# One image's turn in another order: new places for each stage on TensorE, VectorE, ScalarE, GpSimd and the DMA queue

## The chip, the core and the metric

The kernel runs on one core of one Trainium2 chip. The metric is device time in microseconds (us) of one execution. The kernel before was run three times: median 4677.69 us, from 4676.67 to 4680.09. The profile is of another execution of the same program.

## What is computed

32 images of 96 channels and 56 x 56 pixels (3136 tokens) go through two layers. Cut to what matters:

```python
# layer 0
h = conv7x7_depthwise(x) + conv_b                    # first phase of the kernel
h = layernorm_over_channels(h)
x = x + layer_scale * (gelu(h @ w1 + b1) @ w2 + b2)  # 96 -> 384 -> 96
# layer 1
t = tokens(x)
h = relu(bn1(layernorm(t) @ aw1))                    # 96 -> 192
X = fft(h, axis=tokens)
xr = relu(X.real * rd - X.imag * idg + rb)
xi = relu(X.imag * rd + X.real * idg + ib)
t = t + bn2(ifft(xr + 1j * xi).real @ aw2)           # 192 -> 96
t = t + quantized_ffn(layernorm(t))                  # 96 -> 384 -> 96, fp8 products
```

The transform over 3136 tokens is done as two small ones (112 x 28), with a store to DRAM and a load back between them in each direction.

## The kernel before

A first phase (the first 640 us) does the convolution for all images and leaves its output in DRAM; the change does not touch it. The second phase, `image_phase`, is a pipeline over images. One pass of its loop is called a **turn**. In turn n, three images are in work at once: part 1 of image n, part 2 of image n-1, part 3 of image n-2, and the start of image n+1. An image is cut into 7 chunks of 448 tokens (8 chunks in part 2). I write M2/0 for stage M2 of chunk 0. The stages, with the lines of TensorE and of the engine that takes the result:

| part | stages in order, with what the other engines do for them |
|---|---|
| next image | L0S statistics (DVE L809), L0N normalize (DVE L831 h_norm), HT transpose (PE L980, ACT L733) |
| 1 | M1 (PE L987, GELU on ACT L748), M2 (PE L993, residual sum with `x_sb` on DVE L853), T transpose and statistics (PE L999, DVE L809), W1 (PE L1007, ReLU on DVE L875), A outer transform (PE L1015, ACT L756, stored by SP L636) |
| 2 | B inner transform (PE L1026, ACT L767, DVE L892, POOL L712), W (PE L1035, ACT L776), IB inner inverse (PE L1042, ACT L741, stored by SP L655) |
| 3 | AP outer inverse (PE L1049, sum on DVE L903), S2 transpose and statistics (PE L1056, ACT L781, DVE L809), N2 normalize (DVE L831 xn), T2 (PE L1062, ACT L789), F1 (PE L1070, ACT L796), G ReLU and cast (DVE L922, L929), F2 (PE L1077, ACT L801, DVE L934 and L939) |

GpSimd (POOL L683) computes the power that ends each statistics step.

Within a turn the program of every engine is a fixed list. Table `STAGES` gives each stage a first place, a distance from chunk to chunk and a count; `LATER` shifts a stage for one engine; `stages` sorts the steps of each engine by these numbers. Nothing else decides the order: semaphores make a step wait for its data and buffers, and everything behind a waiting step on its engine waits too. TensorE's list also decides which of the 8 PSUM banks each result gets (`banks`).

All DMAs of this phase are issued by one queue, SP, whose list is sorted in the same way. Its steps are: M2 (store the chunk to DRAM, L613), A (store the outer transform, L636), IB (store the inner inverse, L655), FETCH and FETCH NEXT (load `t1_old` for AP, L598). Three larger transfers hang on the last chunk of a step. Behind A/6, SP waits for all stores of A and loads `inner`, the input of the next turn's B, 2016 KB and 336 KB and 42 KB (L646, L647). Behind IB/7 it waits for the stores of IB and loads `back` for the next turn's AP (1176 KB, L665). Behind M2/6 it loads the next image into `x_sb` (1176 KB, L594):

```python
if name == "M2":
    sp.wait_ge(t1_done.sem, t1_done.at(n, c))
    sp.dma_start(t1_dram[...], t1[:, c % 4, :])
    if followed and c == NC - 1:
        load_x()
```

`x_sb` is a single buffer, so its load can start only when M2/6 of this turn is done on DVE. Its first reader is M2/0 of the next turn on DVE, which waits for the load:

```python
if name == "M2":
    if c == 0:
        dve.wait_ge(x_loaded.sem, x_loaded.at(n))
```

At the end of a turn SP stores `out` (L670), and at the start of the next it loads `h` (1176 KB, L605). The turns are start, first, second, a loop of 29 equal turns ("steady"), last, after and end.

Of the kernel before, what the change touches and what calls it, by code (L numbers as in the profile page):

```python
# [20 lines left out]
NC = NQ // CH  # L21
# [3 lines left out]
ND = (NS + CH - 1) // CH  # L25
# [50 lines left out]
def before(n, k, per, ring):  # L76

    if k >= ring:
# [3 lines left out]


STAGES = {
    1: {"M1": (-3, 11.8, NC), "M2": (7, 11.8, NC), "T": (13, 11.8, NC), "W1": (22, 11.8, NC), "A": (27, 11.8, NC)},
    2: {"B": (11, 9.3, ND), "W": (24, 9.3, ND), "IB": (28, 8.8, ND)},
    3: {"AP": (3, 11.5, NC), "S2": (8, 11.5, NC), "N2": (14, 11.5, NC), "T2": (18, 11.5, NC), "F1": (20.5, 12, NC),
        "G": (25, 11.5, NC), "F2": (32, 11.5, NC)},
    "next": {"L0S": (34, 3.4, NC), "L0N": (72, 3.3, NC), "HT": (79, 2.8, NC)},
    "fetch": {"FETCH": (9, 11.5, NC - 3)},  # L90
    "fetch next": {"FETCH NEXT": (78, 1, 3)},
}

LATER = {
    "act": {"W": -0.5, "G": -0.5},
    "dve": {"B": 3, "M2": 2, "T": 2, "W1": 1, "F2": 2, "AP": 1, "S2": 1, "L0N": -1, "W": -2},
    "pool": {"B": 4, "T": 3, "S2": 2, "F1": 1},
    "sp": {"M2": 3},
    "pe": {},
}  # L100

# [1233 lines left out]
```

## Time and profile before

| what | us |
|---|---|
| median of three runs | 4677.69 |
| the profiled execution, its own time | 4678.17 |
| its span, first to last instruction | 4676.4 |
| convolution phase, about | 640 |
| 29 turns of the loop, each | 122.85 |
| PE busy, share of the span | 3989.9 (85%) |
| DVE busy, share of the span | 3461.5 (74%) |
| ACT busy, share of the span | 2285.2 (49%) |
| POOL busy, share of the span | 1390.6 (30%) |

The turn's length is the distance from the first to the last pass of the loop at the store of `out`, over 28. Turns of the loop repeat to a few hundredths of a microsecond, so one turn can be read for all; the text reads the one from about 2056 to 2179 us. Matmuls overlap in the pipeline, so PE's busy time is not work at its peak. Lines of the changed kernel are one higher than those given here, because its table has one line more.

### The profile page before, as it was taken

The numbers are of one execution on the slowest core, as the hardware profiler recorded it, in microseconds if no ns is written. First come the engines' busy times: TensorE is split into PE (matmuls) and PEld (weight loads), VectorE is DVE, ScalarE is ACT, GpSimd is POOL, SyncE is SP. The second block draws the span as 40 slices with busy tenths as digits, with TensorE's granted clock in tenths as the row PEclk, the third lists the DMA queues.
The fourth block names the chain that finished last, engine by engine and source line by source line (L and its number), as shares of the span: only waits on it lengthen the run. The fifth ranks groups of instructions, "written<-read, shape, count | busy, mean of one in ns | idle before, by whom it ended". The sixth has DMA issues, their size and how long they took to land.

```text
span 4676.4 us, 88192 instructions
## 1 busy us (share of the span) xinstructions
PE 3989.9 (85%) x22802; PEld 2808.8 (60%) x22802; DVE 3461.5 (74%) x11833; ACT 2285.2 (49%) x4610; POOL 1390.6 (30%) x1572
## 2 busy tenths in 40 slices
PE   5999969888888888888888888888888888888885
PEld 3444436666666666666666666666666666666664
DVE  2333346788888888888888888888888888888876
ACT  2444424455555555555555555555555555555543
POOL 1111233333332333333333333333333232333331
PEclk8999979999999999999999999999999999999986
DMA  6666524344444444444443333343444444444331
GB/s 172 166 169 172 163 71 107 94 111 115 111 113 113 111 112 115 109 113 115 110 114 105 98 102 107 102 108 105 108 113 114 111 113 114 112 112 113 100 91 49
DMA packets 420416, 532.48 MB, mean 114 GB/s; under 512 B 220047, under 2 KB 378493, under 8 KB 404413
## 3 DMA queue, kind: packets, MB, share of 16 engines
q1 hardware_dynamic: 405920, 510.40, 40.6%
q10 hardware_dynamic: 14272, 20.04, 1.7%
q14 instruction: 199, 1.63, 0.1%
q8 instruction: 25, 0.41, 0.0%
HBM read 295.18 MB, written 235.12 MB: 113 GB/s over the span
## 4 chain that ended last, share of the span: by engine, by line
PE 36%; DVE 30%; issue 12%; ACT 2%; POOL 2%; DVEq 1%; DMA 1%; ACTq 0%; POOLq 0%; SPq 0%
PE psum L993 9%; PE psum L987 7%; PE psum L1026 5%; DVE minus L892 5%; DVE xn L831 4%; DVE h_norm L831 4%; DVE plus L892 4%; DVE stats L809 3%; PE psum L1035 2%; PE psum L1007 2%; DVE act L875 2%; PE psum L1015 2%; PE psum L1049 2%; DVE h L922 1%; PE psum L1062 1%
## 5 line engine op out<-in xcount | busy, mean ns | idle before, releaser
L683 POOL TENSOR_TENSOR scales<-sums,minus_half 112x4 f32<-112x4 f32 (+1 forms) x480 | 636.6, 1355 | 2191.8 <-DVE sums L824 2191.8
L712 POOL TENSOR_TENSOR both<-plus,minus 96x224 f32<-96x224 f32 (+1 forms) x1024 | 618.2, 623 | 587.3 <-DVE minus L892 502.9
L993 PE MATMUL psum<-hid,w_sb 128*96 128x448 f32 x1344 | 592.8, 580 | 6.5 <-ACT hid L748 2.0
L987 PE MATMUL psum<-hn,w_sb 96*128 96x448 f32 x1344 | 557.2, 547 | 8.4 <-ACT h L796 6.9
L767 ACT ACTIVATE uw<-psum,spec 96x224 f32<-96x224 f32 (+1 forms) x1024 | 445.6, 511 | 157.5 <-PE psum L1026 154.9
L386 PE MATMUL c_psum<-c_xt,c_toeplitz 128*112 128x448 f32 x1152 | 476.6, 551 | 50.3 <-ACT c_xt L328 26.9
L414 DVE TENSOR_SCALAR c_h<-c_psum,c_bias 112x448 f32<-112x448 f32 x192 | 199.0, 1036 | 413.1 <-PE c_psum L386 413.1
L892 DVE SCALAR_TENSOR_TENSOR plus<-psum,spec,uw 96x224 f32<-96x224 f32 (+1 forms) x1024 | 426.8, 417 | 63.5 <-ACT uw L767 63.0
L748 ACT ACTIVATE hid<-psum,b_sb 128x448 f32<-128x448 f32 x672 | 419.7, 635 | 104.1 <-PE psum L987 61.9
L892 DVE SCALAR_TENSOR_TENSOR minus<-psum,spec,uw 96x224 f32<-96x224 f32 (+1 forms) x1024 | 425.8, 416 | 0.0
L1035 PE MATMUL psum<-aw_sb,both 96*112 96x96 f32 x3712 | 410.3, 263 | 4.7 <-ACT hid L748 4.7
L1026 PE MATMUL psum<-inner_dft,inner 112*96 112x112 f32 x3712 | 404.1, 261 | 4.8 <-DMA inner<-outer_spectrum 4.8
L1035 PEld LDWEIGHTS psum<-aw_sb,both 96*112 96x112 f32 x3712 | 395.3, 179 | 19.6 <-ACT hid L748 17.8
L1026 PEld LDWEIGHTS psum<-inner_dft,inner 112*96 112x96 f32 x3712 | 389.0, 165 | 23.1 <-issue 14.0
L875 DVE SCALAR_TENSOR_TENSOR act<-psum,scales,below 112x192 f32<-112x192 f32 x896 | 309.2, 406 | 96.4 <-PE psum L1007 88.6
L1062 PE MATMUL psum<-ident,xn 112*96 112x112 f32 x896 | 138.4, 282 | 278.8 <-DVE xn L831 278.8
L1007 PE MATMUL psum<-aw_sb,t 96*112 96x192 f32 x1792 | 343.6, 329 | 35.2 <-DVE t L853 35.1
L987 PEld LDWEIGHTS psum<-hn,w_sb 96*128 96x128 f32 x1344 | 246.2, 191 | 211.6 <-issue 154.8
L993 PEld LDWEIGHTS psum<-hid,w_sb 128*96 128x96 f32 x1344 | 218.5, 176 | 245.7 <-issue 220.6
L809 DVE BATCH_NORM_STATS2 stats<-t_rows 112x6 f32<-112x96 f32 x896 | 164.5, 246 | 253.6 <-ACT t_rows L781 253.6
L1007 PEld LDWEIGHTS psum<-aw_sb,t 96*112 96x112 f32 x1792 | 291.8, 177 | 95.4 <-DVE t L853 53.6
L1015 PE MATMUL psum<-act,outer_dft 113*114 113x192 f32 x1792 | 332.3, 328 | 19.1 <-DVE act L875 19.1
(85 smaller groups left out, 6549.5 us busy)
## 6 DMA issues: line engine op xcount, KB each, us to landing
outer_spectrum<-outer SPq DMA_DIRECT2D x448, 168.0 KB
inner<-outer_spectrum SPq DMA_DIRECT2D x32, 2016.0 KB
c_xpad<-x SPq DMA_DIRECT2D x96, 392.0 KB, 11.2
h_tokens<-c_h SPq DMA_DIRECT2D x24, 1568.0 KB, 8.4
h<-h_tokens SPq DMA_DIRECT2D x32, 1176.0 KB, 13.3
x_sb<-x SPq DMA_DIRECT2D x32, 1176.0 KB, 7.3
residual_stream<-t SPq DMA_DIRECT2D x224, 168.0 KB, 2.1
inner_inverse<-unmixed SPq DMA_DIRECT2D x224, 168.0 KB, 2.3
```

The source lines that it names most:

```text
L386: last = pe.matmul(psum[0:PT, 4 + k % 4, 0:NB * NYB], toeplitz[:, c, half, BR * d:BR * (d + 1), :].rearrange("p t x -> p (t x)"), xt[:, sl ...
L683: nc.gpsimd.tensor_tensor(scales[which][:, at:at + w], su[:, :, 5], minus_half[:, 0:w], ALU.pow).then_inc(ready.sem, 1)
L712: last = nc.gpsimd.tensor_tensor(both[:, c % 2, m, 0:w, k * PT // 2:(k + 1) * PT // 2], half(plus), half(minus), ALU.subtract if k else AL ...
L748: nc.scalar.activation(hid[:, c % 2, m, :], bank("M1", c, m, CW, 128), ACT.Gelu, bias=b1_sb[:, m:m + 1]).then_inc(gelu_done.sem, 1)
L767: last = nc.scalar.activation(uw[:, j % 2, k, 0:w * PT // 2].rearrange("p (s k) -> p s k", s=w), re, ACT.Identity, bias=spec[:, m, shift:s ...
L892: last = nc.vector.scalar_tensor_tensor(out=dst[:, j % 2, k, 0:w * PT // 2].rearrange("p (s k) -> p s k", s=w), in0=im, scalar=spec[:, m, ...
L987: pe.matmul(bank("M1", c, m, CW, 128), w1_sb[:, m * 128:(m + 1) * 128], hn[:, c * CW:(c + 1) * CW], start=True, stop=True).then_inc(m1_mad ...
L993: last = pe.matmul(dst, w2_sb[:, m, :], hid[:, c % 2, m, :], start=(m == 0), stop=(m == KF - 1))
L1007: last = pe.matmul(dst[:, j * H2:(j + 1) * H2], t1[:, c % 4, at:at + PT], aw1_sb[:, :], start=True, stop=True)
L1015: last = pe.matmul(dst[:, j * H2:(j + 1) * H2], outer_dft[:, CH * c + 2 * m + j, :], act1[:, (2 * c + m) % 4, j, :], start=True, stop=True)
L1026: last = pe.matmul(dst[:, s * PT:(s + 1) * PT], inner[:, CH * c + s, m * C:(m + 1) * C], inner_dft[:, :], start=True, stop=True)
L1035: last = pe.matmul(dst[:, s * C:(s + 1) * C], both[:, c % 2, m, s, :], aw2_sb[:, m, :], start=(m == 0), stop=(m == 1))
```

## The change

Only the numbers of the two tables change, and so only the order of each engine's steps (and with TensorE's order the bank of each result). No instruction is added or removed in the loop but a few register operations.

```diff
 STAGES = {
-    1: {"M1": (-3, 11.8, NC), "M2": (7, 11.8, NC), ...
+    1: {"M1": (-0.5, 11.8, NC), "M2": (8.5, 11.6, NC), ...
...
 LATER = {
...
-    "sp": {"M2": 3},
+    "sp": {"M2": 18.0, "FETCH NEXT": 2.0, "IB": -12.5, "A": -9.0, "FETCH": 21.5},
```

On the DMA queue SP, the end of a turn of the loop, before (`t` stands for `t1`, `t_old` for `t1_old`):

```order
L613 DMA residual_stream<-t 96x448
L594 ISA
L594 DMA x_sb<-x 96x3136
L633 REGISTER_ALU
L636 DMA outer_spectrum<-outer 56x768 x2
L636 DMA outer_spectrum<-outer 2x768
L653 REGISTER_ALU
L655 DMA inner_inverse<-unmixed 112x96
L659 ISA
L665 DMA back<-inner_inverse 112x2688
```

Now, the last rows of the turn, from M2/5's store on:

```order
L614 DMA residual_stream<-t 96x448
L634 REGISTER_ALU
L637 DMA outer_spectrum<-outer 56x768 x2
L637 DMA outer_spectrum<-outer 2x768
L642 ISA x2
L647 DMA inner<-outer_spectrum 112x4x192
L647 DMA inner<-outer_spectrum 112x24x192
L648 DMA inner<-outer_spectrum 56x192
L614 ISA
L614 DMA residual_stream<-t 96x448
L595 ISA
L595 DMA x_sb<-x 96x3136
```

M2/6's store and with it the load of `x_sb` stood ahead of A/5, IB/7, the load of `back` and A/6; now they stand behind A/6 and the loads of `inner`. The three FETCH NEXT loads moved from ahead of IB/6 to behind the load of `back`, and M2/5's store from ahead of A/4 to just ahead of A/6.

On VectorE (DVE), the start of a turn of the loop, before: AP/0, M2/0, S2/0, and then the first rows of B/0.

```order
L903 TENSOR_TENSOR t<-psum,t_old 96x448
L846 ISA
L847 ISA
L850 ISA
L851 ISA
L852 ISA
L853 SCALAR_TENSOR_TENSOR t<-psum,b_sb,x_sb 96x448
L809 BN_STATS stats<-t_rows 112x6 x4
```

Now: AP/0, the end of S2/0, M2/0, N2/0, and then B/0 (which stood ahead of N2/0).

```order
L825 SCALAR_TENSOR_TENSOR sums<-sums 112x4
L847 ISA
L848 ISA
L851 ISA
L852 ISA
L853 ISA
L854 SCALAR_TENSOR_TENSOR t<-psum,b_sb,x_sb 96x448
L832 TENSOR_SCALAR xn<-t_rows,sums,scales 112x96 x4
L884 ISA
L886 ISA
L893 SCALAR_TENSOR_TENSOR plus<-psum,spec,uw 96x224
```

M2/0 moved behind S2/0, and N2/0 moved ahead of B/0's eight instructions. In the later chunks N2 moved ahead of G of the chunk before (it stood behind it).

Whole orders, as stages: on DVE a turn began AP/0 M2/0 S2/0 B/0 N2/0 T/0 AP/1 S2/1 M2/1 W1/0 B/1 G/0 N2/1, and now begins AP/0 S2/0 M2/0 N2/0 B/0 AP/1 T/0 S2/1 M2/1 B/1 N2/1 W1/0 G/0. It ended N2/6 L0N/4 T/6 L0N/5 L0N/6 F2/5 W1/6 G/6 F2/6, and now ends N2/6 T/6 G/5 L0N/3 L0N/4 F2/4 L0N/5 W1/6 L0N/6 G/6 F2/5 F2/6. On PE a turn began M1/0 AP/0 M2/0 S2/0 M1/1 B/0 T/0 AP/1 T2/0 M2/1 S2/1, and now begins M1/0 AP/0 S2/0 M2/0 B/0 M1/1 AP/1 T/0 B/1 T2/0 S2/1 M2/1. Between W1/c and the next step that needs its PSUM bank PE had nothing or little to do (W1/1 T/2 adjacent); now M1 stands there for chunks 0 to 4. The seven HT steps, spread over the last part of PE's turn, now stand at its end.

## Rows read from the trace of the kernel before

**Rows 1.** Store of `out`, passes of the loop (count; duration ns; first to last start, us).

```profile
L670 SPq ALU_OP  x29: 41/41/54, 964.3 to 4404.0; - x29
```

**Rows 2.** Busy us per engine in one turn, then in 3.8 us behind PE's wait (PEclk: clock).

```profile
2055.00:2178.00 123.00, 106.65 (x657) 78.18 (x656) 101.71 (x365) 64.20 (x134) 39.16 (x47) 0.99 0.41 109
2076.30:2080.10 3.80, 3.80 (x9) 1.60 (x8) 1.24 (x6) 0.54 (x1) 1.01 (x1) 0.63 1.07 321
```

**Rows 3.** PE's waits in the loop, 940 to 4403 us (total, times, longest).

```profile
PE psum L1062 <- DVE xn L831: 229.1, 85, 4.3
PE psum L999 <- DVE act L875: 92.0, 57, 2.0
```

**Rows 4.** PE in time, T2/0 (start, us, what; in brackets the wait before).

```profile
2075.71 0.95 PE L1062 MATMUL psum<-ident,xn 112*96 112x112 f32 x4 [4.27 <-DVE xn L831]
```

**Rows 5.** DVE in time: four of its waits in this turn (F2/6, AP/0, S2/1, S2/3).

```profile
2061.03 0.33 DVE L934 TENSOR_SCALAR y<-y,fb_q 96x448 f16<-96x448 f16 x1 [1.44 <-ACT y L801]
...
2064.72 0.62 DVE L903 TENSOR_TENSOR t<-psum,t_old 96x448 f32<-96x448 f32 x1 [2.33 <-PE psum L1049]
...
2081.16 0.74 DVE L809 BATCH_NORM_STATS2 stats<-t_rows 112x6 f32<-112x96 f32 x4 [3.36 <-ACT t_rows L781]
...
2118.09 0.74 DVE L809 BATCH_NORM_STATS2 stats<-t_rows 112x6 f32<-112x96 f32 x4 [0.97 <-ACT t_rows L781]
```

**Rows 6.** DVE in time: the end of the turn (G/5, N2/6, L0N/4, T/6, L0N/5, F2/5, W1/6, G/6).

```profile
2171.06 0.82 DVE L922 TENSOR_SCALAR h<-h,fb_q 128x448 f16<-128x448 f16 x3
...
2172.84 1.04 DVE L831 TENSOR_SCALAR xn<-t_rows,sums,scales 112x96 f32<-112x96 f32 x4
2173.80 1.04 DVE L831 TENSOR_SCALAR h_norm<-h,sums,scales 112x96 f32<-112x96 f32 x4
2174.76 0.75 DVE L809 BATCH_NORM_STATS2 stats<-psum 112x6 f32<-112x96 f32 x4
...
2176.20 2.01 DVE L831 TENSOR_SCALAR h_norm<-h,sums,scales 112x96 f32<-112x96 f32 x8
2178.13 0.33 DVE L934 TENSOR_SCALAR y<-y,fb_q 96x448 f16<-96x448 f16 x1
...
2179.32 1.36 DVE L875 SCALAR_TENSOR_TENSOR act<-psum,scales,below 112x192 f32<-112x192 f32 x4
2180.59 0.82 DVE L922 TENSOR_SCALAR h<-h,fb_q 128x448 f16<-128x448 f16 x3
```

**Rows 7.** SP's queue in time: x_sb, IB/7, back, A/6, inner (twice), out.

```profile
2046.50 0.33 SPq L594 DMA_DIRECT2D x_sb<-x  x1
...
2053.92 0.33 SPq L655 DMA_DIRECT2D inner_inverse<-unmixed  x1
2055.51 0.64 SPq L665 DMA_DIRECT2D back<-inner_inverse  x2
2059.38 1.39 SPq L636 DMA_DIRECT2D outer_spectrum<-outer  x3
2064.03 0.87 SPq L646 DMA_DIRECT2D inner<-outer_spectrum  x2
2064.95 4.75 SPq L647 DMA_DIRECT2D inner<-outer_spectrum  x1
2069.98 0.35 SPq L670 DMA_DIRECT2D out<-result  x1
```

**Rows 8.** DMA issues of the page: count, KB each, median us from issue to landing.

```profile
h<-h_tokens SPq DMA_DIRECT2D x32, 1176.0 KB, 13.3
x_sb<-x SPq DMA_DIRECT2D x32, 1176.0 KB, 7.3
out<-result SPq DMA_DIRECT2D x32, 1176.0 KB, 9.0
```

**Rows 9.** Turn "second", ahead of the loop: loads of inner (SP), and PE's B/1 behind them.

```profile
733.32 0.85 SPq L646 DMA_DIRECT2D inner<-outer_spectrum  x2
...
745.63 3.30 PE L1026 MATMUL psum<-inner_dft,inner 112*96 112x112 f32 x16 [3.73 <-DMA inner<-outer_spectrum]
```

More of the change, by code:

```diff
@@ L84 @@
 STAGES = {
[L85 to L91, printed above, removed]
+    1: {"M1": (-0.5, 11.8, NC), "M2": (8.5, 11.6, NC), "T": (15.0, 11.2, NC), "W1": (23.0, 11.8, NC),
+        "A": (26.5, 12.1, NC)},
+    2: {"B": (9.0, 8.6, ND), "W": (22.5, 9.1, ND), "IB": (29.0, 9.0, ND)},
+    3: {"AP": (2.0, 11.5, NC), "S2": (8.0, 11.5, NC), "N2": (11.0, 12.1, NC), "T2": (18.0, 10.9, NC),
+        "F1": (22.0, 11.3, NC), "G": (24.0, 11.9, NC), "F2": (36.0, 11.8, NC)},
+    "next": {"L0S": (36.0, 3.7, NC), "L0N": (70.0, 3.3, NC), "HT": (93.5, 1.0, NC)},
+    "fetch": {"FETCH": (-12.0, 10.9, NC - 3)},
+    "fetch next": {"FETCH NEXT": (79.5, 0.8, 3)},
 }
 LATER = {
-    "act": {"W": -0.5, "G": -0.5},
-    "dve": {"B": 3, "M2": 2, "T": 2, "W1": 1, "F2": 2, "AP": 1, "S2": 1, "L0N": -1, "W": -2},
-    "pool": {"B": 4, "T": 3, "S2": 2, "F1": 1},
-    "sp": {"M2": 3},
+    "act": {"W": -1.0, "S2": -1.0, "F1": -1.0, "HT": 1.0, "M1": -1.0, "T2": 0.5, "B": -0.5},
+    "dve": {"B": 4.5, "M2": 1, "T": 2.0, "W1": 1.0, "F2": 8.5, "AP": 2.0, "S2": 1.0, "L0N": 5.5, "L0S": -10.5, "G": 1.0, "N2": 0.5},
+    "pool": {"B": 5.0, "S2": 0.5, "L0S": -0.5},
+    "sp": {"M2": 18.0, "FETCH NEXT": 2.0, "IB": -12.5, "A": -9.0, "FETCH": 21.5},
     "pe": {},
```

## The prediction

> **What bounds the kernel now.** I first read the length of a turn from the store of `out`: (4404.0 - 964.3) / 28 = 122.85 us [rows 1]. 29 such turns are 3563 us of the 4676, so a microsecond per turn is 29 us, and the rest of the program counts little. Then the busy time of one turn by engine [rows 2]: PE 106.65, DVE 101.71, ACT 64.20 and POOL 39.16 of 123. PE and DVE are each near the turn's length, and neither fills it. Then who waits for whom: PE's largest waits in the loop are T2 for N2 on DVE, 229.1 us, and T for the bank that W1's ReLU empties, 92.0 us [rows 3]. In order of time most of the first lies at the start of the turn, 4.27 us ahead of T2/0 [rows 4]. DVE in the same turn shows eight waits of about a microsecond or more, the first 1.44 ahead of F2/6, the last 0.97 ahead of S2/3, the largest 3.36 ahead of S2/1; together 16.4 us, all within 57 us of each other [rows 5]. So the first half of a turn is a relay between PE and DVE in which each often waits for the other, and the second half runs with DVE always busy. What an order can win lies in the first half.
>
> **What the change takes away.** With N2/0 ahead of B/0, T2/0 no longer waits for B/0's eight instructions; with S2/0 sent early, and other work between AP/c and S2/c, DVE has less to wait for at S2/1 and S2/2; with M1 behind W1 on PE, T's wait for the bank is covered. I followed the new lists by hand with the durations above. After M2/0 I find on DVE only one wait of about 1.3 us, at S2/1, whose transpose stands behind B/1 on PE and behind B/1's work on ACT (it can be 0, and it was 3.36, my two bounds). DVE then works through: it is the bound, since PE has about 16 us of its turn free [rows 2]. DVE's occupied time in a turn is at least the busy 101.7 and at most 122.85 - 16.4 = 106.4. I take 105.0, nearer to the upper end, because the gaps between dependent small instructions come again in any order.
>
> **What the change puts in its place.** DVE's M2/0 reads `x_sb`. In SP's list the load of `x_sb` now stands behind A/6 and the loads of `inner`. Before, it was issued at 2046.50 and landed in 7.3 [rows 7, 8], near 2053.8; the M2/0 that reads it comes behind AP/0 at 2064.72 [rows 5], so it was hidden with at least 11 us to spare. I now place it, counting from the end of G/6 on DVE (2059.6 in this turn, one turn back from the end of the last of [rows 6]).
>
> 1. *A/6.* W1/6 now ends ahead of L0N/6 and G/6, before it stood right ahead of G/6. So A/6's store, at 2059.38 or -0.2 before [rows 7], comes one L0N earlier (0.96, [rows 6]): at -1.2. The loads of `inner` follow when A's stores have landed: 2064.03 - 2059.38 = 4.65 later [rows 7]. That gives +3.4 as the earliest time.
> 2. *What is in the queue ahead of it.* `back` is issued 1.59 behind IB/7's store [rows 7]. IB/7 on PE follows T2/6, which waits for N2/6. From the end of N2/6 to the end of G/6 DVE now does T 1.44, G 1.78, three L0N at 0.96, F2 1.19, W1 1.27 and G 1.8 [rows 6] and one more L0N that is moved there, 0.96: 11.3 us. IB/7's store came 2.9 us behind N2/6 before (2053.92 against 2051.03, one turn back from [rows 6]); A/5 and F1/6 now stand between, 1.6 us more. So its store is at -11.3 + 4.5 = -6.8, and `back` at -5.2. `back` and A/6 together took 2064.03 - 2055.51 = 8.5 us to the loads of `inner` [rows 7], which gives +3.3. But three loads of `t1_old` and M2/5's store, 4 x 168 KB, are now in the queue between them: nothing if they hide, at most 3.4 us at the rate at which `inner` landed in the turn "second" (2394 KB in 12.3 us, [rows 9]). I take 2.0. `inner` is issued at +5.3 (bounds 3.4 and 6.7).
> 3. *The load of x.* SP's issue of `inner` took until 2069.98, when `out` could go: 5.95 us [rows 7]. M2/6's store adds 0.5, so `x_sb` is issued at +11.7. `out` in that place landed 9.0 after its issue [rows 8], behind the rest of `inner`; 168 KB more ahead of it add 0.9. So x lands at +21.6. Bounds: 7.3 as it lands alone and 13.3 as `h` lands today from the place behind [rows 8], with the bounds of step 2: +17.1 and +26.4.
>
> The Trainium skill, DMA: Bandwidth & Descriptors, "Queues, rings and completion order", says that descriptors of one queue are consumed in ring order on each DMA engine, but that completion is not first in, first out per issuing engine, and that a copy need not use all 16 rings. By that x could land in the 7.3 us of a free queue, which is the second rival below; the median of `out` today, 9.0, speaks for waiting behind `inner`.
>
> **The sum.** Without the wait, M2/0 would start near +8.7: M1/0, AP/0 and S2/0 stand ahead of it. With it, DVE starts M2/0 at 21.6 + 0.1. Ahead of M2/0 in DVE's turn are F2/5, F2/6 (1.2 each), AP/0 (0.6) and S2/0 (1.4), 4.4 us that now lie inside the wait, so 105.0 - 4.4 = 100.6 are left, plus 1.3 at S2/1. The turn is 21.7 + 100.6 + 1.3 = 123.6 us, 0.75 more than now; 29 turns make 21.8. The change gives back at the load of x what it wins at N2 and S2. Behind 4.27 us of waiting PE was granted 0.63 of full clock for 3.8 us [rows 2], between its levels of 1.2 and 2.4 GHz, 1.4 us of work lost; that will happen behind the new wait too. I cost it at nothing, as PE has time to spare against DVE there; without that cover it is 1.4 a turn.
>
> Outside the loop: in the turn "second" the same load is late by some 13 us, of which 3.7 are waited there already for `inner` [rows 9]: +9. The turns "first", "last" and those behind take a little of the better order; I put 2 us. Together +7. DMAs that are moved otherwise: FETCH NEXT now stands behind `back`, and t1_old lands near +2, ahead of AP/0 at about +5; the stores of M2 go out up to one chunk later, and their buffers come round after four. Both cost nothing unless SP's list gets later by another 3 us.
>
> 4678.2 (the profiled execution's own time) + 21.8 + 7 = **4707 us**. The median of the three runs stands 0.5 below that execution.
>
> **The rivals.**
>
> - *The load of x is not late* (M2/0 is served as before). Then the turn keeps only the waits ahead of M2/0 that I find: 0.3 at F2/6, 2.3 at AP/0 as today [rows 5], 1.5 more for S2/0 and M2/0, and 1.3 at S2/1. 105.0 + 5.4 = 110.4 us, 12.45 less; 29 turns give 361, so about 4317. For it: all gains above are real waits in the trace. Against it: the list puts the issue of x behind 2394 KB, with an issue time of 5.95. It would need a load that lands by +8.7, three microseconds ahead of its issue by step 3. Chance 0.12.
> - *x overtakes in the queue.* It lands 7.3 us after its issue, at +19.0; the turn is 121.0, 1.85 less, and the time 4678 - 54 + 7 = 4631. For it: 7.3 is what it takes where the queue ahead is short [rows 8], and its few long rows may find room beside those of `inner`. Against it: `out`, as large, needs 9.0 in this place. The Trainium skill's rule named above is of this kind. The point from which it decides: x landing before +20.85 makes the turn shorter than now. Chance 0.15.
> - *x shares the engines with out and h*, which SP issues right behind it. It lands as `h` does, 13.3 after its issue, at +25.0; the turn is 127.0, and the time 4678 + 120 + 7 = 4805. Chance 0.15.
>
> **How the numbers follow.** My forecast has 0.58: x lands between +19.5 and +23.7, the turn is between 121.5 and 125.7, the time between 4646 and 4768. Within this case 0.13 lies below the time of now by more than 0.2% (9 us, about what a measurement of this kernel can tell from no change), 0.10 within, and 0.35 above. So faster is 0.13 + 0.12 + 0.15 = 0.40, the same 0.10, slower 0.35 + 0.15 = 0.50. The range goes from 4600, below the second rival, to 4830, above the third: it leaves out the first rival, 0.12, and some 0.07 at its ends.
>
> **What would show it.** Right: DVE's M2/0 (L854 there) shows a wait of 10 to 14 us in each turn of the loop, ended by the load of `x_sb`; that load is issued some 6 us behind the loads of `inner`; the waits of T2 for N2 and of T for W1's ReLU are mostly gone from PE's list; and DVE is busy without a wait of over a microsecond from S2/1 to F2/5. PE waits at T/0 (L1000), behind M2/0, and its clock falls behind that. Wrong: no wait at M2/0 and a turn near 110, or a turn whose length follows another load (`inner` at B/1, `back` at AP/0), or DVE waiting again in the second half because PE or ACT comes late there.

## The result, and the profile after

| kernel | median us | runs | ratio to before |
|---|---|---|---|
| before, in the same session | 4678.77 | 4 (4676.67 to 4680.09) | |
| changed | 4858.7 | 4 (4855.52 to 4864.99) | 1.0387, interval 1.0369 to 1.0405 |

The change costs 180 us, where 29 were forecast. The profiled execution took 4860.98 us (span 4859.2), 182.8 more than that of before. The turn first, as in [rows 1]: the store of `out` in the changed kernel, passes of the loop:

```profile
L671 SPq ALU_OP  x29: 41/41/54, 978.2 to 4586.6; - x29
```

(4586.6 - 978.2) / 28 = 128.87 us, 6.02 more than before. 29 turns make 174.6 of the 182.8; 8.2 lie outside the loop. Single turns vary by more than hundredths: from one store of `out` to the next it takes 121.9 to 123.5 us in the loop before and 125.5 to 130.4 in the loop after. So a turn read below is one sample, and what is given "a turn" is a mean.

Who waits for whom in the loop of the changed kernel, 1000 to 4500 us (total us, times, longest), to be held against [rows 3]:

```profile
DVE t L854 <- DMA x_sb<-x: 372.4, 27, 14.3
...
PE psum L1000 <- DVE t L854: 227.7, 27, 9.2
...
PE psum L1057 <- DVE t L904: 97.3, 54, 3.2
DVE t L904 <- issue: 95.6, 27, 3.9
DVE stats L810 <- ACT t_rows L782: 83.1, 54, 1.9
...
DVE h_norm L832 <- PE psum L981: 56.9, 26, 2.9
...
DVE t L854 <- PE psum L994: 17.1, 54, 1.1
```

T2's wait for N2, 229.1 us before, is gone from the list, as intended. In its place stands M2/0 on DVE, which waits 13.8 us a turn for `x_sb`, and PE's T/0 behind it. The queue SP in the turn that follows the end of G/6 (2124.1 us), for [rows 7]:

```profile
2120.38 1.49 SPq L599 DMA_DIRECT2D t_old<-residual_stream  x3
2122.12 0.34 SPq L614 DMA_DIRECT2D residual_stream<-t  x1
2123.25 1.42 SPq L637 DMA_DIRECT2D outer_spectrum<-outer  x3
2129.80 0.87 SPq L647 DMA_DIRECT2D inner<-outer_spectrum  x2
2130.72 4.93 SPq L648 DMA_DIRECT2D inner<-outer_spectrum  x1
2135.85 0.35 SPq L614 DMA_DIRECT2D residual_stream<-t  x1
2136.38 0.33 SPq L595 DMA_DIRECT2D x_sb<-x  x1
2136.96 0.33 SPq L671 DMA_DIRECT2D out<-result  x1
```

`x_sb` is issued 12.3 us behind the end of G/6, and its median landing, from the page's DMA issues ([rows 8]), is 11.1 us later:

```profile
h<-h_tokens SPq DMA_DIRECT2D x32, 1176.0 KB, 17.6
x_sb<-x SPq DMA_DIRECT2D x32, 1176.0 KB, 11.1
```

DVE in the same turn, every wait of half a microsecond or more from L0N/4 on (for [rows 5]): L0N/4, AP/0, S2/0, M2/0, S2/1.

```profile
2116.91 1.05 DVE L832 TENSOR_SCALAR h_norm<-h,sums,scales 112x96 f32<-112x96 f32 x4 [1.44 <-PE psum L981]
...
2130.63 0.62 DVE L904 TENSOR_TENSOR t<-psum,t_old 96x448 f32<-96x448 f32 x1 [3.72 <-issue]
2132.83 0.74 DVE L810 BATCH_NORM_STATS2 stats<-t_rows 112x6 f32<-112x96 f32 x4 [1.58 <-ACT t_rows L782]
2147.52 1.01 DVE L854 SCALAR_TENSOR_TENSOR t<-psum,b_sb,x_sb 96x448 f32<-96x448 f32 x1 [13.20 <-DMA x_sb<-x]
2155.90 0.74 DVE L810 BATCH_NORM_STATS2 stats<-t_rows 112x6 f32<-112x96 f32 x4 [1.50 <-ACT t_rows L782]
```

The waits at AP/0 and S2/0 cost nothing here, because x lands later than both. Busy time per engine in one whole turn, then in 4 us behind the wait (PEclk is the first of the last three numbers), for [rows 2]:

```profile
2055.00:2183.87 128.87, 109.79 (x668) 82.66 (x668) 103.17 (x368) 64.58 (x134) 38.74 (x47) 0.93 0.40 105
2151.00:2155.00 4.00, 4.00 (x23) 4.00 (x24) 3.30 (x14) 1.63 (x4) 2.98 (x5) 0.53 0.96 197
```

So the forecast mechanism is there and larger than forecast. Open are two things: that it is x's load and nothing else in SP's list, and where the turn's other 3.5 us come from.

### The profile page after: what moved, and what is told of

Its sections match the earlier page's. It is cut to its first block and busy times, and to the rows that moved or that the text cites. A ratio compares the mean times of both kernels' runs of the same rounds, so it can differ in the third digit from the quotient of the medians.

```text
span 4859.2 us, 88540 instructions
## 1 busy us (share of the span) xinstructions
PE 4087.7 (84%) x22802; PEld 2932.6 (60%) x22802; DVE 3471.5 (71%) x11833; ACT 2276.7 (47%) x4610; POOL 1377.5 (28%) x1572
## 5 line engine op out<-in xcount | busy, mean ns | idle before, releaser
L684 POOL TENSOR_TENSOR scales<-sums,minus_half 112x4 f32<-112x4 f32 (+1 forms) x480 | 626.8, 1308 | 1994.0 <-DVE sums L825 1993.9
L854 DVE SCALAR_TENSOR_TENSOR t<-psum,b_sb,x_sb 96x448 f32<-96x448 f32 x224 | 230.4, 1029 | 491.0 <-DMA x_sb<-x 439.2
L1027 PE MATMUL psum<-inner_dft,inner 112*96 112x112 f32 x3712 | 455.9, 281 | 56.5 <-DVE minus L893 46.1
L1027 PEld LDWEIGHTS psum<-inner_dft,inner 112*96 112x96 f32 x3712 | 430.8, 181 | 106.1 <-DVE minus L893 54.1
L797 ACT CAST h<-psum 128x448 f16<-128x448 f32 x672 | 314.1, 541 | 275.3 <-PE psum L1071 275.3
L1000 PE MATMUL psum<-ident,t 96*112 96x96 f32 x896 | 131.4, 276 | 324.0 <-DVE t L854 267.6
L1016 PE MATMUL psum<-act,outer_dft 113*114 113x192 f32 x1792 | 343.5, 336 | 0.1
L387 PEld LDWEIGHTS c_psum<-c_xt,c_toeplitz 128*112 128x112 f32 x1152 | 194.4, 180 | 217.3 <-issue 212.1
## 6 DMA issues: line engine op xcount, KB each, us to landing
x_sb<-x SPq DMA_DIRECT2D x32, 1176.0 KB, 11.1
```

The lines of the kernel that those rows point to most:

```text
L387: last = pe.matmul(psum[0:PT, 4 + k % 4, 0:NB * NYB], toeplitz[:, c, half, BR * d:BR * (d + 1), :].rearrange("p t x -> p (t x)"), xt[:, sl ...
L684: nc.gpsimd.tensor_tensor(scales[which][:, at:at + w], su[:, :, 5], minus_half[:, 0:w], ALU.pow).then_inc(ready.sem, 1)
L1016: last = pe.matmul(dst[:, j * H2:(j + 1) * H2], outer_dft[:, CH * c + 2 * m + j, :], act1[:, (2 * c + m) % 4, j, :], start=True, stop=True)
L1027: last = pe.matmul(dst[:, s * PT:(s + 1) * PT], inner[:, CH * c + s, m * C:(m + 1) * C], inner_dft[:, :], start=True, stop=True)
```

## The experiments

The time of a turn is worked out for each as above, from its first and last pass at the store of `out`. "A single run" is one execution beside the kernel before and has no interval.

### Is it the load of x?

**e1, x early.** In the changed kernel, M2's seven stores on SP, and with the last of them the load of x, go back to an early place.

```diff
-    "sp": {"M2": 18.0, "FETCH NEXT": 2.0, ...
+    "sp": {"M2": -1.0, "FETCH NEXT": 2.0, ...
```

> The changed kernel with one number of SP's list put back: M2 at -1.0 instead of +18.0, so that M2/6's store and the load of x_sb stand ahead of A/5 and IB/7 again; all other engines as in the changed kernel. Theory (the late load of x costs the time, the new order of the engines by itself gains): the 13.8 us wait of DVE's M2/0 goes, and what is left is a wait of 3 to 5 us of PE's B/1 for inner, which is issued near +5.7 us behind G/6 and lands 12.3 us later; the turn is 114 to 119 us, the time 4420 to 4570 us. Rival (the loss lies in the new order of the engines, with HT at the turn's end, and the wait for x only took the place of others): the wait at M2/0 goes, but other waits come for it, the turn stays above 124 us and the time above 4720 us.

4569.8 us, ratio to before 0.9764 (0.9748 to 0.978); the turn is 119.28. x lands 7.6 us after its issue and M2/0 no longer waits for it. PE waits 1.4 us a turn for `inner`, where 3 to 5 were expected at B/1. DVE's two largest waits in the loop of e1, 1100 to 4200 us, and the one at L0N/4:

```profile
DVE t L904 <- issue: 128.2, 24, 6.4
DVE stats L810 <- ACT t_rows L782: 103.0, 52, 3.3
...
DVE h_norm L832 <- PE psum L981: 46.1, 23, 2.9
```

One number in one table turns 3.9% slower into 2.4% faster. The first row, AP/0 with no releaser, is taken up in e16.

**e10, x alone.** The same with the stores of M2 left late:

```diff
-                        if followed and c == NC - 1:
-                            load_x()
...
+                    if name == "A" and c == NC - 2 and followed:
+                        sp.wait_ge(t1_done.sem, t1_done.at(n, NC - 1))
+                        load_x()
```

> The changed kernel with the load of x_sb alone moved ahead, to right ahead of A/5 (it still waits for M2/6 on DVE); M2's seven stores, FETCH, IB and A keep the late places of the change. e1 moved the load together with M2's stores and gave 4569.8. Theory (of SP's list, the place of x's load is the part that costs): turn 118.8 to 120.2 us, 4555 to 4597 us, and no wait at M2/0 for x. Rival (the late stores of M2, or the t_old loads among the large transfers, carry a part of the loss of their own): over 4640 us.

4583.9 us, ratio 0.9793 (0.9778 to 0.9808), turn 120.06. The load of x by itself carries 8.8 us of a turn; the stores of M2 at most the 0.8 between e10 and e1.

**e2 and e3, the two halves of the change.** e2 is the kernel before with SP's new list. e3 is the changed kernel with SP's list of before. Both sort SP's steps by the other kernel's tables:

```diff
-    return {engine: order(later) for engine, later in LATER.items()}
+    return {engine: order(QUEUE_LATER["sp"], QUEUE_STAGES) if engine == "sp" else order(later)
+            for engine, later in LATER.items()}
```

> The kernel before, with SP's list alone in the order of the changed kernel. Theory: M2/0 on DVE waits for x here too, from about +7 us to +22 us behind G/6, and nothing is gained elsewhere; the turn is 132 to 139 us, the time 4940 to 5150 us. Rival: the queue's order costs little, the turn is within 2 us of the kernel before, the time below 4740 us.

> The changed kernel, with SP's list alone in the order of the kernel before (x_sb ahead of A/5, FETCH NEXT ahead of IB/6, M2's stores early). Theory: as with x loaded early alone, and the loads of inner come 2 to 2.5 us earlier, since 672 KB less stand in the queue ahead of A/6; the turn is 112 to 117 us, the time 4360 to 4510 us. Rival: above 4720 us.

e2: 5255.7 us in a single run, turn 142.01, worse than expected. DVE's wait for x there, 1100 to 4800 us, is 16.7 us a turn (433.3 / 26):

```profile
DVE t L874 <- DMA x_sb<-x: 433.3, 26, 18.2
```

e3: 4507.2 us in a single run, at the upper end of what was expected, turn 117.35. **e9** is the same program, timed:

> The same program as e3 (new order on the four engines, SP's list as before the change), now timed for an interval. One look gave 4507.2 us. Expected: median 4500 to 4515, ratio to the kernel before 0.962 to 0.965. If that look was an outlier, the median lies over 4530.

4515.4 us (4501.6 to 4519.5, 5 runs), ratio 0.9642 (0.9629 to 0.9655): at the upper edge of what was expected; it beats both kernels by more than any other version. So the new order on the four engines alone gains 3.6%, and SP's new list costs 19.2 us a turn under the old order and 11 under the new.

**e7 and e14, x in the middle.** e7 puts M2/6's store and x right ahead of A/6's store (SP's "M2" at 11.9). e14 puts x behind A/6's stores, ahead of the wait for them and the loads of `inner`:

```diff
                     if name == "A" and c == NC - 1:
+                        if followed:
+                            sp.wait_ge(t1_done.sem, t1_done.at(n, NC - 1))
+                            load_x()
```

> The changed kernel with M2 on SP at 11.9 instead of 18.0: M2/6's store and the load of x_sb stand right ahead of A/6 and the loads of inner, instead of right behind them. Theory (transfers of this queue land one after the other): x lands at +6 to +9 us and M2/0 waits little, but inner is issued 4 to 5 us later, at +10, so B/0 and B/1 wait instead; the turn is 119 to 124 us, the time 4570 to 4720 us. Rival (transfers overtake, only the time of issue counts): neither waits, and the time is below 4500 us.

> The changed kernel with the load of x_sb between A/6's stores and the loads of inner (M2/6's store stays behind inner). x is then issued at about +0.7 us from the end of G/6 instead of +12.3. Theory (x lands near +9 to +11, about when DVE comes to M2/0, and inner, one x later in the queue, lands 4 us later at most, partly hidden): turn 119.5 to 123 us, 4575 to 4690 us. Rival (x holds up A/6's stores on the shared DMA engines, so that inner is issued 10 us or more behind A/6 and PE waits at B as in e7): 4700 to 4770 us.

e7: 4728.2 us in a single run, over what was expected, turn 124.75. e14: 4571.8 us, ratio 0.9769 (0.9752 to 0.9786), turn 119.35, a little under what was expected and as good as x early. SP's queue in e7, then in e14:

```profile
2072.85 0.32 SPq L595 DMA_DIRECT2D x_sb<-x  x1
2073.28 1.53 SPq L637 DMA_DIRECT2D outer_spectrum<-outer  x3
2084.87 0.87 SPq L647 DMA_DIRECT2D inner<-outer_spectrum  x2
```

```profile
2148.79 1.42 SPq L635 DMA_DIRECT2D outer_spectrum<-outer  x3
2150.41 0.35 SPq L595 DMA_DIRECT2D x_sb<-x  x1
2155.51 0.85 SPq L648 DMA_DIRECT2D inner<-outer_spectrum  x2
```

With x ahead of A/6's small stores, SP gets to `inner` 11.6 us behind them, since it waits until they have landed. With x right behind them it takes 6.7, as without x (6.55). Two neighbouring places differ by 5.4 us a turn (M2/6's small store goes with x in e7 and stays behind `inner` in e14).

**e15, the same on top of e9.** SP's old list, x moved as in e14.

> e3 / e9 (new order on the engines, SP's old list, 4515.4 us) with the load of x_sb moved from behind M2/6 to between A/6's stores and the loads of inner, out of the way of IB/7's store and the load of back. Theory (back is issued 1.6 us behind IB/7 instead of 4.0, AP/0 waits 2 us less, and inner's later landing hides): 4435 to 4490 us. Rival (x's 1176 KB only change victims: inner or x itself is late): 4530 to 4640 us.

4529.2 us (4513.1 to 4533.1), ratio 0.9679 (0.9663 to 0.9695), no gain on e9 and at the edge of the rival. `back` does come early, but AP/0 waits all the same. In e3, ahead of AP/0, SP's queue and DVE read:

```profile
2119.06 0.33 SPq L676 DMA_DIRECT2D inner_inverse<-unmixed  x1
2123.10 0.64 SPq L686 DMA_DIRECT2D back<-inner_inverse  x2
```

```profile
2131.78 0.62 DVE L924 TENSOR_TENSOR t<-psum,t_old 96x448 f32<-96x448 f32 x1 [3.12 <-PE psum L1070]
```

and in e15:

```profile
2125.12 0.33 SPq L677 DMA_DIRECT2D inner_inverse<-unmixed  x1
2126.99 0.64 SPq L687 DMA_DIRECT2D back<-inner_inverse  x2
```

```profile
2140.94 0.62 DVE L925 TENSOR_TENSOR t<-psum,t_old 96x448 f32<-96x448 f32 x1 [6.17 <-issue]
```

The issue of `back` went from 4.0 us behind IB/7's store to 1.9, but AP/0 now waits 6.2 us for something the trace does not name.

### Where do the other 3.5 us of a turn come from?

**e11, does h take x's bandwidth?** The load of `h` behind the first load of `t_old`.

```diff
                         fetch_t1(n, c + 3)
+                        if kind == "steady" and c == 0:
+                            load_h()
```

> The changed kernel with the load of h behind the first load of t_old in SP's list instead of right behind the store of out; x_sb, inner and out keep their places. Tests why x landed 11.1 us after its issue and not 9.9. Theory (x shares the DMA engines with h, issued 1.6 us behind it): x lands 9 to 10 after its issue, the turn is 126.8 to 127.8, 4798 to 4830 us. Rival (x waits for what is ahead of it, inner and M2/6's store, and h takes nothing from it): landing 11 or more, 4848 us or more.

4849.5 us (4842.4 to 4860.2), turn 128.71; x still lands 11.1 us after its issue. The rival holds: `h` takes nothing from x.

What x does wait for can be read from the DMA packets in the traces, which differ in size from one transfer to another (means over 20 turns). In the changed kernel x's first row begins 4.7 us after its issue, while the last rows of `inner` begin (5.2), and x lands 6.3 us behind its first row. In the kernel before and in e9, with little ahead in the queue, the first row begins after 1.1 us and x lands 6.2 to 6.3 behind it (7.5 in e14, where `inner` is issued while its rows run). So the place behind `inner` costs x its late start; its own rows take as long here, where rows of `out` follow them, as there. The store of `out`, in that place in the kernel before, begins its rows after 4.2 us and lands only 4.8 behind that.

**e12, L0N/4's wait.** HT spread again as before the change.

```diff
-    "next": {..., "HT": (93.5, 1.0, NC)},
+    "next": {..., "HT": (79, 2.8, NC)},
...
-    "act": {..., "HT": 1.0, "M1": -1.0, ...
+    "act": {..., "M1": -1.0, ...
```

> The changed kernel with the seven HT steps on PE and ACT spread over the last part of the turn as before the change (places 79, 2.8), x_sb still late. Tests the wait that the prediction missed, L0N/4 on DVE for the buffer that HT/0 empties, 2.1 us a turn by the changed kernel's waits. Theory (that wait lies in DVE's chain and adds to the turn): 4790 to 4815 us. Rival (DVE would wait about as long for something else there; with x early the same edit gave only 7 us): 4840 to 4862 us.

4891.3 us, ratio 1.0451 (1.0435 to 1.0467), turn 129.64: slower, beyond both. DVE's waits, 1000 to 4500 us:

```profile
DVE t L854 <- DMA x_sb<-x: 366.3, 27, 14.2
DVE t L904 <- issue: 132.2, 27, 5.3
...
DVE act L876 <- PE psum L1008: 37.9, 27, 1.4
```

The wait of `h_norm` is gone, and W1's on PE has come (1.4 a turn). Over 22 turns the stretch from M2/0 to the end of the next G/6 is 104.8 us, only 0.4 less than in the changed kernel, so the wait was hardly a cost of its own: it showed that PE is late at the end of the turn. The loss is ahead of M2/0: x is issued 13.5 us behind G/6 instead of 12.1. **e4**, the same edit on e1, said so too:

> x loaded early as in the first kernel of this set, and HT spread over the end of PE's turn again (first place 79, distance 2.8, as before the change) instead of standing in a row at its end. Theory: DVE's L0N/3 to L0N/4 no longer waits about 2 us a turn for the buffers that HT/0 empties, and F2/6 and M1/0 find PE free; 1 to 2.5 us a turn less than the first kernel of this set, 30 to 75 us. Rival: HT between the other steps holds PE up as much as it frees DVE, within 10 us of the first kernel or slower.

4562.8 us in a single run, 7 below e1, whose own runs differ by as much. The stretch from M2/0 to the end of G/6 is 105.3 us in both.

**e13, e17, e18, the low clock.** Extra matmuls (their results are overwritten) keep PE busy while it waits for M2/0. e17 and e18 differ only in the 7 and 11:

```diff
                         dst = bank("AP", c, 0, CW, C, "dve")
+                        if kind == "steady" and c == 1:
+                            for _ in range(11):
+                                pe.matmul(dst, ident[0:C, 0:C], hn[:, 0:CW], start=True, stop=True)
```

> The changed kernel with 14 matmuls more per turn on TensorE (96x448, into T/0's bank, their result overwritten by T/0) between AP/1 and T/0, where TensorE waits 8.6 us for M2/0. At 0.54 us each they take 7.6 us and fit in the wait; they keep the engine busy, so that the granted clock should stay near 1.00 behind the wait where it was 0.50 to 0.53 for some 10 us. Theory (the low clock makes S2/1 and the steps behind it late for DVE): turn 126.4 to 127.9 us, 4787 to 4831 us. Rival (DVE's own work covers it, the prediction's cost of nothing holds): 4848 to 4870 us.

> The changed kernel with 7 matmuls more per turn on TensorE (96x448, 1.0 us each as measured in e13, into AP/1's bank right ahead of AP/1, which overwrites them), so that they lie inside the 8.6 us in which TensorE waits for M2/0. The granted clock should stay near 1.00 there instead of 0.50. Theory (the low clock makes the steps behind the wait late for DVE): turn 126.4 to 127.9 us, 4787 to 4831 us. Rival (DVE covers it, the prediction's cost of nothing holds): 4848 to 4870 us.

> e17 with 11 matmuls more per turn instead of 7. In e17 seven took 5.42 us (0.77 each), TensorE still waited 3.0 us for M2/0, and its clock still fell to 0.50 behind that wait; eleven take 8.5 us and fill the wait. Theory (the low clock makes the steps behind the wait late for DVE): clock near 1.00 behind T/0, B/0 on TensorE 1.7 us instead of 3.3, turn 126.4 to 127.9 us, 4787 to 4831 us. Rival (DVE covers it): the clock stays high and the time does not follow, 4848 to 4870 us.

e13 does not test it: its matmuls stood in T/0's PSUM bank, which is the bank of M2/0, so they ran behind the wait. Its 5116.2 us say what 14 us more on PE cost there: 8.8 a turn. e17: 4857.1 us, no change; 3.0 us of the wait stayed empty, and the clock still fell. e18: 4839.8 us (4834.7 to 4850.2), ratio 1.0353 (1.0335 to 1.0371), turn 128.07. The stretch behind the wait in e17, then the wait and the stretch behind it in e18:

```profile
2148.00:2152.00 4.00, 4.00 (x23) 4.00 (x24) 3.11 (x14) 1.83 (x4) 3.09 (x5) 0.51 0.83 176
```

```profile
2128.00:2137.00 9.00, 9.00 (x30) 4.20 (x29) 1.87 (x5) 0.86 (x2) 0.00 (x0) 1.00 1.03 319
2137.00:2144.00 7.00, 5.61 (x39) 3.85 (x38) 6.17 (x28) 2.73 (x6) 3.56 (x5) 1.00 0.84 169
```

In e18 the clock stays at 1.00 there and the turn is 0.8 us shorter (0.65 by the medians): less than the theory's 1.0 to 2.5, more than the rival's nothing. DVE's waits in e18, 1000 to 4500 us:

```profile
DVE stats L810 <- ACT t_rows L782: 72.0, 54, 1.8
DVE h_norm L832 <- PE psum L981: 45.9, 25, 2.8
```

Each is 11 us less than in the changed kernel; the 22 in 27 turns are the 0.8.

### What the order can still gain

**e6, N2 alone.** The kernel before with N2's new place on DVE and nothing else.

```diff
-    3: {..., "N2": (14, 11.5, NC), ...
+    3: {..., "N2": (11.0, 12.1, NC), ...
...
-    "dve": {..., "W": -2},
+    "dve": {..., "W": -2, "N2": 0.5},
```

> The kernel before with one stage moved alone: N2 on DVE at the changed kernel's places (ahead of B/0, and ahead of G of the chunk before). Theory (N2 behind B/0 and behind G was the main wait of the old order): PE's 4.27 us at T2/0 and 2.61 us at T2/1 fall by 2 to 3 us each, the clock does not fall behind them, and DVE's 3.36 us at S2/1 go with them; 3 to 6 us a turn less, 4500 to 4590 us. Rival: N2 waits for GpSimd there and delays B/0 by as much; within 25 us of the kernel before.

4632.5 us in a single run, turn 121.38: between what theory and rival expected. T2's wait falls as it should, and another takes part of its place. PE's waits, 1100 to 4200 us:

```profile
PE psum L993 <- DVE stats L809: 85.6, 51, 3.0
...
PE psum L1062 <- DVE xn L831: 49.6, 51, 1.3
```

M2 on PE now waits for the bank that T's statistics empty, since T moved behind N2 on DVE. One stage moved alone gains 1.5 us of the 5.0 to 5.5 that the whole order gains.

**e5 and e8, earlier IB and later B.** e5 is e3 with W and IB closer together (on SP's list too, where IB's distance goes from 8.8 to 8.2), so that `back` comes earlier. e8 is e5 with B later by a step.

```diff
-    2: {"B": (9.0, 8.6, ND), "W": (22.5, 9.1, ND), "IB": (29.0, 9.0, ND)},
+    2: {"B": (9.0, 8.6, ND), "W": (22.5, 7.95, ND), "IB": (29.0, 7.58, ND)},
```

> The new order of the engines with the old queue order (4507 us in one look, turn 117.35 us, DVE waiting 4.45 us at AP/0 because back lands late behind x_sb, PE waiting 1.45 us at B/1 for inner), and in addition W and IB closer together (distance 7.95 and 7.58 on PE and ACT), so that W/7 and IB/7 stand ahead of T/6 and T2/6, and IB/7 ahead of A/5 on SP. Theory (what is left of the loss at a turn's start is the queue: x, back and inner landing in a row): back is issued near -15 instead of -6 us, AP/0 no longer waits for it, inner comes 2 to 4 us earlier; 2 to 4 us a turn less, 4390 to 4455 us. Rival: W and IB ahead of their data hold up PE, or the waits at AP/0 are PE's own; 4500 us or more.

> The kernel with back early, and in addition B on PE at 11.2 + 9.0 c instead of 9.0 + 8.6 c (with DVE, ACT and GpSimd shifted so that they keep their places for B to within a step), so that B/1 stands behind M2/1. Theory: B/1's wait for inner and S2/1's wait behind it go; 0.5 to 2 us a turn less than the kernel with back early, 15 to 60 us. Rival: the later chunks of B come late for DVE and W; slower than the kernel with back early.

Both lose: e5 4603.6 us (ratio 0.9834, 0.9818 to 0.985), e8 5566.4 in a single run. In e5, W waits for the bank that ACT's copy of IB empties; in e8, W stands in PE's list ahead of its data. PE's waits, e5 and then e8, 1100 to 4200 and to 4800 us:

```profile
PE psum L1056 <- ACT unmixed L762: 69.8, 52, 1.6
```

```profile
PE psum L1056 <- POOL both L733: 514.2, 99, 6.7
```

A fixed list has no slack: a step moved without its feeders waits in front of everything behind it.

**e16, the wait without a releaser.** e15 with two turns written out in each pass of the loop.

```diff
-            with eng.Fori(2, NB - 1) as n:
-                turn("steady", n)
+            turn("steady", 2)
+            with eng.Fori(0, (NB - 4) // 2) as g:
+                turn("steady", g * 2 + 3)
+                turn("steady", g * 2 + 4)
```

> e15 with two turns written out in each pass of the loop (one turn ahead of the loop, then 14 passes of two), so that each engine jumps back half as often; orders, buffers and data are the same. In e15 DVE waits 6.4 us (173.0 us in 27 turns) ahead of AP/0, its first step of a turn, with no releaser in the trace, while an 8 KB packet on the queue named instruction ends some 2.5 us ahead of AP/0. Theory (the wait is the jump back, its code being loaded through DMA engines that are full of back, x_sb and inner): the wait is found in every second turn only, 14 times 5 to 6 us less, 4435 to 4475 us against 4529. Rival (it is data or a buffer): every turn keeps it, 4510 to 4545 us.

4618.3 us, ratio 0.9866 (0.985 to 0.9883): outside both expectations. Waits in its loop, 1000 to 4300 us, and AP/0 on DVE behind a jump, in the middle of the pass and behind the next jump:

```profile
PE psum L1011 <- issue: 140.6, 13, 12.2
DVE t L927 <- PE psum L1073: 225.3, 36, 16.1
```

```profile
2175.59 0.62 DVE L927 TENSOR_TENSOR t<-psum,t_old 96x448 f32<-96x448 f32 x1 [14.47 <-PE psum L1073]
...
2285.20 0.62 DVE L927 TENSOR_TENSOR t<-psum,t_old 96x448 f32<-96x448 f32 x1 [1.29 <-PE psum L1073]
...
2418.08 0.62 DVE L927 TENSOR_TENSOR t<-psum,t_old 96x448 f32<-96x448 f32 x1 [15.67 <-PE psum L1073]
```

On DVE the wait without a releaser is gone; in the middle of a pass AP/0 waits 1.3 us. But PE now has such a wait, 10 to 12 us ahead of M1/0, its own first step, in 13 of 27 turns, which is once per pass; DVE's row behind the jump is its consequence. From AP/0 to AP/0 the turn with no jump ahead of it takes 2285.20 - 2175.59 = 109.6 us and the other 132.9. So the waits stand at the jump back and not at data. That they are the loading of code is read from the packets of the queues named "instruction". For DVE, in the loops of the changed kernel, e1, e7, e14 and e15, an 8 KB packet ends 2.0 to 2.1 us ahead of AP/0 (medians of 24 turns). For PE, e16 has a queue of 16 KB packets that the changed kernel and e15 do not have in their loops, and in each of the 13 waits one of them ends 1.4 to 1.8 us ahead of M1/0. Its row among the DMA queues (packets, MB, share), 1000 to 4200 us:

```profile
q8 instruction: 184, 3.01, 0.4%
```

The Trainium skill, Runtime: NRT & Kernel Launch, "Instruction fetch mechanics", says that a taken branch whose target is not in the two pages of code at hand forces a fetch before execution goes on. It gives 2048 instructions as what PE's instruction memory holds. The trace fits that size: one turn holds 1336 matmuls and weight loads of PE, and PE shows no such wait; two turns hold 2672, and it does. No run sets the size of the body between the two.

## Why the prediction was wrong, step by step

The mechanism and the side of the sign were as forecast; the size was not. The gap is 4861 - 4707 = 154 us.

1. *A/6's store*, "at -1.2": it came at -0.9.
2. *inner*, "at +5.3 (bounds 3.4 and 6.7)": at +5.7. Holds; the 6.55 us between A/6's store and `inner`, 4.65 before, are the t_old loads and M2/5's store that the step named.
3. *x*, "issued at +11.7 ... lands at +21.6": issued at +12.3, and M2/0 started at +23.4 instead of 21.7. The term that was off is the landing, 11.1 us after the issue instead of 9.9, inside its bounds. It was taken from `out`, a store, which lands 4.8 us behind its first row; x, a load of the same size, takes 6.3. Of the rival in which x shares the engines with `out` and `h`, e11 excludes `h`, and the packets show no loss to `out`: x's rows take 6.2 to 6.3 where no `out` follows. The place in the queue sets the rest: 7.4 us in e9, 10.0 in e14, 11.1 here. The rival "x overtakes" is refuted: x's rows began as `inner`'s ran out. The Trainium skill, DMA: Bandwidth & Descriptors, "Queues, rings and completion order", allows a later transfer to finish before an earlier one. No run here shows that for x. Steps 1 to 3 miss by 1.7 us a turn, 49 us in all.
4. *The sum*, "100.6 are left, plus 1.3 at S2/1": **this is the step that failed.** M2/0 to the end of the next G/6 took 128.87 - 23.4 = 105.45 us instead of 101.9: 3.55 a turn, 103 us in all. I found "only one wait" behind M2/0. The trace has 2.1 us at L0N/4 (56.9 / 27), 1.7 at S2/1 (mean of 22 turns) where I put 1.3, and 0.6 at M2 of two later chunks (17.1 / 27). DVE is occupied for 105.7 us (128.87 less the 23.2 a turn of its five waits shown) instead of 105.0, 0.3 of that in this stretch. The L0N wait needs HT/0 to have emptied a buffer, and HT had moved to PE's end; I listed that move in the order and left its consequence out. e12 and e4 show that it is hardly a cost of its own: with HT earlier, DVE waits for W1. PE is late at that place, whichever of the two steps stands there, and I had asked of PE only whether its sum fits ("16 us of its turn free"), not whether it fits at the end of the turn. My own signs of being wrong had named it: "DVE waiting again in the second half because PE or ACT comes late there". The late x is not what makes this stretch long. Over 22 turns the stretch is 105.2 us in the changed kernel, and 105.3, 105.6, 104.5 and 105.3 in e1, e10, e14 and e3, where x is early or nearly so; L0N/4 waits there too, 1.8, 1.5 and 1.4 us a turn in the first three, and S2/1 waits longer in e1, e10 and e3 than here.
5. *The low clock*, "I cost it at nothing ... without that cover it is 1.4 a turn": 0.8 a turn by e18, 23 us in all (0.65 and 19 by the medians), part of step 4's miss. The cover was half there: behind the wait, at 0.50, B/0 alone took 3.30 us on PE where it takes 1.70 in the kernel before.
6. *Outside the loop*, +7: 8.2.
7. *The gain in the same change*, "the change gives back at the load of x what it wins": right, and e3 and e9 size it. The rival "x not late" gave 4317 us and a turn of 110.4; the real kernels without that wait are at 117.4 to 120.1. They wait 3.4 to 6.5 us a turn at AP/0, where I put 2.3, and again at S2 and M2. The 2.3 was not PE's alone either: in the kernel before, too, an instruction packet ends 1.7 us ahead of AP/0. Both the forecast and that rival err to the same side, by too few waits.
8. *The range* went to 4830 and held the landing's bounds for x, but none for the number of waits found by hand, which was the larger unknown.

Not settled: what makes PE late for L0N/4 and W1/6 at the end of the turn. No run made PE's list shorter there.

## What to carry to other kernels

When a table of places sorts a DMA queue too, read first what hangs on the moved step: here a 1.2 MB load hung on a 168 KB store, and one number in one table was the difference between 3.9% slower and 2.4% faster. On one queue, a load with a far deadline goes well ahead of the small stores whose landing the queue waits for, or right behind them and ahead of the large loads (e1 and e14 are equal); right ahead of them it cost 5.4 us a turn more (e7 against e14). For a transfer's landing, take a row of one that goes the same way: a store stood in for a load here. And a fixed order simulated finds the large wait and misses the small ones that follow it, so give the sum a margin for them on the slow side.

## What the runs showed of the hardware

- Behind the jump back at the end of a loop pass DVE stood idle, with no releaser in the profile, for 3.5 us (changed kernel) to 7.2 us (e7) ahead of its first step, which began 2.0 to 2.1 us behind the end of an 8 KB instruction packet. PE stood 10 to 12 us once its body was two turns long (e16).
- On one queue x's rows began as the rows of `inner` ahead of it ran out, 4.7 us after the issue; with little ahead they began after 1.1. The load of 1176 KB landed 6.2 to 6.3 us behind its first row (7.5 with `inner` issued meanwhile, e14), the store of the same size 4.8.
- PE's granted clock fell to 0.50 (1.2 GHz) behind a wait of which 3.0 us were left empty (e17) as well as behind 8.6, and stayed at 1.00 when the wait was filled with work (e18). The price was 0.65 to 0.8 us a turn.
- SP itself stood 4.9 us at one issue of `inner`, and 7.5 in e15, so a load placed behind it is late before it is in the queue.
